# Both halves of an output projection ahead of the next block's row transposes, in a fused adaLN, scan-attention and expert kernel

## What is computed

```python
h = _layernorm(x) * (1 + ca) + sa
# attention half, on h
xn = _rmsnorm(h, rms_mix_w)
g, v, d = xn @ Wg.T + bg, xn @ Wv.T + bv, xn @ Wd.T + bd
a = 0.001 + 0.998 * sigmoid(d)
h = h + scan_causal(sigmoid(g) * tanh(v), a)      # state = a * state + x_scan
xn = _rmsnorm(h, rms_ffn_w)
h = h + (silu(xn @ W_gate.T) * (xn @ W_up.T)) @ W_out.T
x = x + ga * h
# expert half
h = _layernorm(x) * (1 + cb) + sb
scores = softmax(h @ router_w)                    # top 2 of 8 experts
y = sum over the two of weight * ((gelu(h @ w1[e]) * (h @ v1[e])) @ w2[e]) + bias
x = x + gb * y
```

## Time and profile before

| | |
|---|---|
| runs (us) | 980.4, 978.73, 978.65 |
| median (us) | 978.73 |
| span of the profiled execution, first to last instruction (us) | 975.1 |
| TensorE busy, share of the span | 858.6 us, 88% |
| VectorE, ScalarE, GpSimd busy | 64%, 37%, 46% |
| expert half begins (first tile's transposes) | 444.18 us |

### The profile page before, as it was taken

The page is one execution under the profiler, slowest core; times in us unless marked ns, Lnnn a source line. Parts: engine busy times, 40 slices in busy tenths (PEclk is TensorE's granted clock), DMA queues, the critical chain, the costliest instruction groups (busy, mean ns, idle before and its releaser), DMA issues.

```text
span 975.1 us, 21422 instructions
## 1 busy us (share of the span) xinstructions
PE 858.6 (88%) x5443; PEld 787.8 (81%) x5444; DVE 623.3 (64%) x1688; ACT 362.9 (37%) x658; POOL 444.4 (46%) x438
## 2 busy tenths in 40 slices
PE   5558899898989988506999999999999999999994
PEld 2447888787878887506999999999999999999994
DVE  3775798878887857562556556565565656655553
ACT  2735365636546333212224224242242324222221
POOL 1424365665858557660334335343343433443333
PEclk9869999999999988757999999999999999999998
DMA  7000401202021122364223324233242222212121
GB/s 260 22 22 1 135 25 65 88 23 87 33 69 52 45 81 71 131 201 136 35 44 104 57 40 124 44 91 66 44 124 35 41 33 43 34 33 44 33 40 20
DMA packets 48928, 65.22 MB, mean 67 GB/s; under 512 B 4928, under 2 KB 43968, under 8 KB 48896
## 3 DMA queue, kind: packets, MB, share of 16 engines
q1 hardware_dynamic: 30704, 41.83, 15.0%
q0 software_dynamic: 13392, 18.27, 9.4%
q10 hardware_dynamic: 4800, 4.74, 1.5%
HBM read 41.28 MB, written 23.54 MB: 66 GB/s over the span
## 4 chain that ended last, share of the span: by engine, by line
PE 64%; DVE 9%; POOL 9%; issue 7%; ACT 6%; DMA 3%; ACTq 0%; DVEq 0%; SPq 0%; POOLq 0%
PE ps L1306 13%; PE ps L1308 13%; PE ps L1307 13%; PE ps L1339 6%; PE ps L455 4%; PE ps L456 4%; PE ps L457 4%; POOL routed L1170 3%; POOL hid_lo L370 3%; PE ps L1353 2%; ACT squares L653 2%; PE ps L1315 2%; DMA out_rows<-y_moe,tok_moe 1%; DVE h_sb L885 1%; ACT xn_sb L669 1%
## 5 line engine op out<-in xcount | busy, mean ns | idle before, releaser
L1306 PE MATMUL ps<-w_moe_hi,xT_moe_hi 128*128 x568 | 190.5, 335 | 1.3 <-DVE xT_moe_lo L1437 1.3
L1308 PE MATMUL ps<-w_moe_lo,xT_moe_hi 128*128 x568 | 184.9, 326 | 0.0
L1307 PE MATMUL ps<-w_moe_hi,xT_moe_lo 128*128 x568 | 184.9, 326 | 0.0
L1492 POOL TENSOR_TENSOR y_moe<-y_moe 128x256 f32<-128x256 f32 x71 | 51.6, 727 | 261.6 <-DVE y_moe L1456 261.6
L1396 ACT ACTIVATE hidT_hi<-ps 128x768 fp32r<-128x768 f32 x71 | 57.6, 812 | 184.8 <-PE ps L1339 184.8
L1498 POOL DMA_INDIRECT out_rows<-y_moe,tok_moe x71 | 111.0, 1564 | 33.6 <-issue 33.2
L1306 PEld LDWEIGHTS ps<-w_moe_hi,xT_moe_hi 128*128 128x128 f32 x568 | 107.9, 190 | 1.7 <-issue 1.7
L1306 PE MATMUL ps<-w_moe_hi,hidT_hi 128*128 x355 | 106.1, 299 | 2.3 <-DVE hidT_hi L1465 2.3
L1307 PEld LDWEIGHTS ps<-w_moe_hi,xT_moe_lo 128*128 128x128 f32 x568 | 107.8, 190 | 0.0
L1308 PEld LDWEIGHTS ps<-w_moe_lo,xT_moe_hi 128*128 128x128 f32 x568 | 107.6, 189 | 0.0
L1456 DVE SCALAR_TENSOR_TENSOR y_moe<-ps,gate_moe,gates 128x256 f32<-128x256 f32 x142 | 62.1, 479 | 64.9 <-PE ps L1353 63.0
(11 more groups left out here) (197 smaller groups left out, 2078.2 us busy)
## 6 DMA issues: line engine op xcount, KB each, us to landing
raw<-in_w SPq DMA_DIRECT2D x8, 1408.0 KB
x_moe<-routed SPq DMA_DIRECT2D x74, 132.5 KB, 2.6
raw<-in_w SPq DMA_DIRECT2D x8, 640.0 KB
x_sb<-in_x SPq DMA_DIRECT2D x8, 512.0 KB, 4.7
x_again<-in_x SPq DMA_DIRECT2D x8, 512.0 KB, 3.8
out_rows<-x_again ACTq DMA_DIRECT2D x8, 512.0 KB, 3.1
wmod_sb<-in_wmod SPq DMA_DIRECT2D x1, 1536.0 KB, 6.5
gu_raw<-in_gu_t SPq DMA_DIRECT2D x1, 1536.0 KB, 13.5
```

The costliest lines, as they stand in the source:

```text
L1306: pe.matmul(dst, a_hi, b_hi, start=first, stop=False)
L1307: pe.matmul(dst, a_lo, b_hi, start=False, stop=False)
L1308: return pe.matmul(dst, a_hi, b_lo, start=False, stop=last)
```

## The change

TensorE issues both halves of the output projection before it transposes the rows of the next block and ranks the tokens, and VectorE evicts both halves before xn_lo and slots. The tests on r stay the same, so this holds in steps 2 to 9, also in steps 7 to 9, in which there is no next block.

```diff
@@ -591,12 +591,11 @@
                     if r == 2:
                         pe.wait_ge(w_lo[2], 1)
                     ffn_out(adding, 0)
+                    ffn_out(adding, 1)
                 if r + 1 < NBLK:
                     xn_transposes(q.near(1))
                 if r >= 3:
                     rank_tokens(routing)
-                if 2 <= r < NBLK + 2:
-                    ffn_out(adding, 1)
                 if r == 1:
                     pe.wait_ge(w_lo[1], 1)
                 for m in range(KFA):
@@ -1034,6 +1033,7 @@
                     keep_last(q)
                 if add_on:
                     add_ffn(adding, 0)
+                    add_ffn(adding, 1)
                 if r == -1:
                     first_rows(1)
                     last_rows()
@@ -1043,7 +1043,6 @@
                 if route_on:
                     slots(routing)
                 if add_on:
-                    add_ffn(adding, 1)
                     gate_xo(adding)
                 if ffn_on:
                     hidden(ffn, 0)
```

## The result

The changed kernel takes 988.5 us (median of 4 runs, 987.73 to 990.03) against 978.69 us of the kernel before beside it (975.67 to 980.4): a ratio of 1.0109, 95% interval 1.0095 to 1.0123. It is slower, as forecast, but by 9.8 us where 4.8 were forecast, and beyond the range's upper end of 987.8. The profiled execution took 988.66 us with a span of 986.9, so 1.8 us lie outside the span; span against span the change costs 11.8 us. The two differences don't agree because the profiled execution of the kernel before was faster than its median, and its runs spread along with the mean clock granted to them: of its 23 runs beside e1 and e2, nine at a mean of 0.941 or 0.942 took 975.9 to 976.9 us and nine at 0.936 or 0.937 took 978.8 to 981.6, while the profiled execution was at 0.942.

A forecast was written before the change was run, and what follows sets the result against it. The expert half's start, set by GpSimd's last scatter, was taken to bound the gain, with a ring through other engines setting each step. -5.0 + 9.8 = +4.8 us on the 975.1 span, plus 3.6 outside: 983.5 us, range 979.2 to 987.8.

The forecast's parts named there:

- Step 2: Before routing, the moved half fills TensorE's 2.50 us wait and ends the low clock; the rest comes 4.0 us earlier.
- T(3): Start of TensorE's row transposes in step 3 (T: the same in any step); forecast 151.8, 1.3 us earlier.
- The old wait: TensorE's idle time before the row transposes, for ScalarE's xn_sb, 1.62 to 3.30 us in steps 3 to 6; forecast gone.
- a new one comes at the xn2 transposes: Steps 3 to 6: TensorE would wait 2.2 us there for ScalarE's xn2, which follows GpSimd's rms_2.
- the mark at T + 4.3: Steps 3 to 6: GpSimd's mark, released by slots, still comes 4.3 us after the row transposes start; extra eviction covered.
- I take no loss: Steps 4 to 6: the new 2.2 us wait would not lower TensorE's clock; stated bound 1.4 us per step.
- C: Rival: the new waits lower the clock, adding 3 x 1.4 us, 987.7 us; chance 0.10.
- -5.0 us at the h2 transposes of step 7: Gain accumulated by the steps before: these transposes at 304.6 instead of 309.64, with a period of 42.4 us.
- +9.8 us for steps 7 to 9: No next block, ranks behind both halves: slots and its chain later, +2.1, +3.4 and +4.3 us after slack.
- A: Rival: the filled waits stay filled, TensorE gains all its waits and the low clock, 970.5 us; chance 0.05.
- B: Rival: the delay in steps 7 to 9 is hidden, only -5.0 us is left, 973.7 us; chance 0.07.
- D: Rival: one tail term is covered and the steady part is a little better, +0.5 us, 979.2 us; chance 0.12.

The follow-up runs named there:

- e1: The change on both engines in steps 2 to 6 alone, steps 7 to 9 in the order of the kernel before: 976.94 us, ratio 0.9984 to the kernel before.
- e2: The change on both engines in steps 7 to 9 alone, steps 2 to 6 as in the kernel before: 991.95 us, ratio 1.0135.
- e4: The change in TensorE's order alone, VectorE as in the kernel before: 980.48 us, ratio 1.0028 to the kernel before.
- e3: The changed kernel with gate_xo moved on VectorE behind hidden unit 0 where one exists: 986.46 us, ratio 1.0087 to the kernel before.
- e6: e5 plus, in steps 3 to 6, ranks between quarters of TensorE's second half and slots ahead of VectorE's evictions and xn_lo: 964.42 us, ratio 0.9848.
- e7: e6 plus, in steps 7 to 9, ranks between quarters of the first half and slots ahead of the evictions: 962.93 us, ratio 0.9846.
- e5: TensorE's part of the change only in steps 2 to 6, VectorE as in the kernel before: 972.08 us, ratio 0.9928 to the kernel before.

## Why the prediction was right and wrong

- **Step 2 and T(3).** Right. The h2 transposes of step 3 come at 134.9 in place of 138.9 (-4.0), T(3) at 151.72 (151.8 foretold).
- **The old wait goes, a new one comes at the xn2 transposes, norm2_centre waits for the residual.** Right in kind: in all of steps 3 to 6. In size: 2.6 to 2.9 us instead of 2.2. e4, without the slow mark, has 1.7 to 1.9. VectorE's new waits for the residual, a sign I had named, sum up to 28.5 us in seven steps (before, there was one, of 3.3 us):

```profile
DVE stats L863 <- POOL x_again L1149: 28.5, 7, 7.4
```

- **"From the mark to the end of the residual are 8.1 us", the mark at T + 4.3.** Here a step failed. The mark came at T + 4.2, but I took the operations of GpSimd's queue at their old durations though I had moved VectorE's work beside them. The mark now takes 1.1 us. Only part of that is new: one scatter was 0.5 us longer before (1.45 against 0.96), for the same reason. Step 4, the one where the clock held, gives the size that is left: period 42.72 against 42.4, so 0.3 us per step. (Against e4, where neither mark nor scatters are held up for long, it is 0.8.) e3 shows that the position of gate_xo causes it.
- **"I take no loss" for the clock.** Wrong, and the dearer failure in the steady part. The periods at 43.65 and 43.59 against 42.72 give 0.9 us for steps 3 and 5 each; step 6 gives 0.8 (26.53 us from T to the h2 transposes, against 25.69 in step 4). It is 2.6 us in all, less than 1.4 in each of three steps. But 1.4 was no bound: it assumed a stretch of 2.8 us, and from the windows above some 1.7 us of TensorE's work are lost in each of the three (an estimate: length times what the granted clock lacks to 1.00). How the step took up the other 0.8 wasn't followed; step 4 has one wait that a later TensorE would not have, 0.3 us for the bank of the last gate_up unit (216.76). C's sign, a clock below 1.00 between T + 15 and T + 20, is there in steps 3, 5 and 6. I had counted low clock after three of five waits and yet put only 0.10 on rival C: by those rows it was the likelier case. The Trainium skill, "TensorE: Matmul & The Clock Gate", section "HAM oscillation — how this bites in real kernels", says that a wait which makes the clock gate close costs a slow start again at every tile. The trace agrees in three of four steps. The new waits of 2.6 to 2.9 us are shorter than the old ones of 3.2 to 3.3, and are followed by the low clock about as often.
- **-5.0 us at the h2 transposes of step 7.** It was -1.4. The miss of 3.6 is the two items above: T(4) to T(6) and the transposes are late by 1.2, 1.5, 2.7 and 3.6 us, that is 1.2, 0.3, 1.2 and 0.9 per step; 0.3 of each (0.1 of the last) is the mark, the rest the clock.
- **+9.8 us for steps 7 to 9.** Right for what it described, in part by luck. e4 has this tail with marks of 0.2 us: 303.42 to its mark of step 9 (398.94) are 95.5 us, before 85.6 (309.64 to 395.20), so +10.0. Two things cancel in it. From the h2 transposes of step 8 to its mark e4 loses 5.2 us (18.75 against 13.59), 0.9 more than the 36 matmuls: "TensorE follows this chain and does not lead it" fails there, since chosen_b was ready at 356.07 in the kernel before and TensorE got to the ranks only at 358.60, so that its low clock counts. And the slacks hid 0.6 us more than the sum had. In the changed kernel it is 97.7 us, +12.1; 2.1 of the 2.2 more arise between the marks of steps 7 and 9 (322.45 to 398.94 in e4, 76.5 us; 327.36 to 405.91 in the changed kernel, 78.6), about what two marks longer by 0.9 us make. The mark of step 9 itself adds another 0.9 behind it.
- **The sum.** -1.4 + 12.1 + 0.9, and 0.2 up to the first transposes, is +11.8 between the spans, where -5.0 + 9.8 was forecast, a miss of 7.0. Of this the slow mark is some 3.7 (1.0 in steps 3 to 6, 1.8 and 0.9 in the tail) and the clock of steps 3, 5 and 6 is 2.6; either alone would have stayed inside the range. The base was also off: I put the 3.6 us between the median of the runs and the profiled span down to start and end of the program. After, these are 1.8 us; the other 1.8 were the profiled execution being faster than the median. That the time was missed by only 5.0 us, 988.5 for 983.5, is due to this error, which went the other way.
- **The rivals.** A (waits stay filled) and B (tail hidden) are refuted, D too. C was right in kind, and its 987.7 us close, though by luck: of its 4.2 us for the clock steps 3 to 6 show 2.6, and the slow mark makes up the rest and more. That e6 reaches 964.4 us shows rival A's 970.5 to be no fantasy, but for another order.

What stays open: why one of four nearly equal waits left the clock alone, and why the low clock of step 8 ended earlier in the kernel before, e3 and e7 than in the other traces. That the low clock costs 0.9 us a time is read from steps with it and without it; no run changed the clock alone.

## What to carry to other kernels

Filling an engine's wait with work from behind it gains little while a ring through other engines sets the period (0.7% in e5, and nothing clear with VectorE's part in e1): find the instruction that releases the ring's slowest queue (here slots and its mark) and move that one forward too (1.5% in e6). Ask the same of the last turns of a software pipeline by themselves: where no next block exists there is no wait to fill, and a small instruction put behind 36 matmuls delays the chain by all of them. When an instruction moves, look at what now runs beside it on the engine that shares its memory path, and where a loop shows the low clock after most of its waits, take it into the forecast.

## What the runs showed of the hardware

- **One VectorE operation with two inputs in SBUF, gate_xo, holds up GpSimd.** It (128x1024 with itself and the gates, 1.22 us) made the mark last until 0.05 us after its own end (199.53 + 1.10 against 199.36 + 1.22): 1.1 us for a 0.2 us operation, in all of steps 3 to 9. An indirect DMA's issue that starts 0.4 to 0.9 us after gate_xo began takes 1.13 to 1.67 us instead of 0.96 to 0.98, in e3, e4, e6 and before, and ends 0.82 to 0.86 us behind gate_xo; in step 4 of e3 at 202.78 against 201.92. One that had started first is not held up, nor is one that starts in gate_xo's last 0.2 us: in step 4 before, the third scatter ran from 202.78 to 203.74, in 0.96 us, though gate_xo began at 203.43. In step 7 before, scatter and gate_xo both began at 327.78 and took 0.96 and 1.26 us. The evictions, with one input in PSUM, ran beside the mark and scatters of e4 without this; they are also half as long, and no run had a long one from PSUM or a short one from SBUF. The Trainium skill, "SBUF — State Buffer", section "Who interferes with whom", gives the rule: the two engines share a pair of ports, and an operation of VectorE with both inputs in SBUF keeps out a GpSimd operation that reads SBUF for its whole duration. The trace agrees for the mark, with the number above. The page supposes that descriptor generation is not touched by such an operation; the scatters here are.
- **The clock after short waits.** In e4, waits of 1.94, 1.91, 1.84 and 1.67 us were followed by the low clock once, after the second:

```profile
167.20:170.00 2.80, 2.78 (x17) 1.00 0.00 0
...
209.10:212.00 2.90, 2.82 (x13) 0.66 0.00 0
...
251.70:254.00 2.30, 2.23 (x14) 1.00 0.00 0
```

  In the changed kernel it was three of four after 2.6 to 2.9 us, before the change two of three after 3.2 to 3.3. In e5, whose steps 2 to 6 are those of e4, waits of 1.93, 1.89, 1.87 and 1.65 us were followed by it once, after the first (0.71 from 167.1 to 173.0). The length of the wait alone doesn't decide it.
